# Four graph-network layers on one core: the first layer's weighed messages are made by one-hot matmuls beside the mixing, scattered as rows and summed from plain transfers

## The reference

```
src, dst: 53125 edges (25000 both ways and 3125 loops), sorted by dst
xn  = layernorm(x)
# graph part
h   = xn @ W.T + b
agg = segment_sum(edge_weight[:, None] * h[dst], src, 3125)
x  += elu(agg)
# mixing part
q, k, v = xn @ Wq + bq, xn @ Wk + bk, xn @ Wv + bv     # 8 heads of 32
kv, k_sum = sum over nodes of phi(k) v, phi(k)          # phi(t) = t + 1 or exp(t)
out = (phi(q) kv / (phi(q) k_sum + 1e-6)) @ Wo + bo
y   = layernorm(xn + out) * g1 + b1n
x  += layernorm(y + relu(y @ W1 + b1) @ W2 + b2) * g2 + b2n
```

## Time and profile before

| | us |
|---|---|
| three executions | 5759.25, 5759.92, 5763.4 |
| profiled execution, its span (the page gives no other time for it) | 6101.2 |
| span less the median of the timed executions | 341 |
| from the start to the ELU of the first layer, in the profiled execution | 1508 |
| PE, DVE, POOL, ACT busy over the span | 4335.5, 3233.1, 2977.7, 1242.5 |

### The profile page before, as it was taken

How to read it: one execution, slowest core, us unless ns; L and a number is a source line. 1 busy time by engine, 2 the same in 40 slices (tenths; PEclk the granted TensorE clock), 3 DMA queues, 4 the chain that set the end, 5 groups by cost and what they waited for, 6 DMA issues and landing times. The chain is left out here.

```text
span 6101.2 us, 68061 instructions
## 1 busy us (share of the span) xinstructions
PE 4335.5 (71%) x17944; PEld 3114.6 (51%) x17944; DVE 3233.1 (53%) x7722; ACT 1242.5 (20%) x3067; POOL 2977.7 (49%) x2938
## 2 busy tenths in 40 slices
PE   0298855555987677763985957888489996777764
PEld 0246543333676454432454845566367774566554
DVE  6324544445111666776985155788732224567752
ACT  0022210000322211110123321100033333333221
POOL 1446666665021388873873536676200005666434
PEclk9988876566988776565996977888789998988867
DMA  5100013333211599885743234444300003222234
GB/s 157 39 19 2 2 39 92 91 91 75 91 35 51 163 291 294 273 270 144 240 129 101 73 106 108 111 111 111 75 8 0 0 2 105 79 85 87 65 108 123
DMA packets 402554, 617.08 MB, mean 101 GB/s; under 512 B 79785, under 2 KB 293694, under 8 KB 401829
## 3 DMA queue, kind: packets, MB, share of 16 engines
q0 software_dynamic: 127136, 331.96, 19.3%
q1 hardware_dynamic: 271940, 278.07, 14.5%
q10 hardware_dynamic: 3154, 3.20, 0.2%
HBM read 482.93 MB, written 130.68 MB: 101 GB/s over the span
## 5 line engine op out<-in xcount | busy, mean ns | idle before, releaser
L877 POOL DMA_INDIRECT m_rows<-support,far_at x440 | 447.7, 1018 | 991.7 <-POOLq L126 744.5
L3966 POOL DMA_INDIRECT g_sp_rows<-h,src_at x440 | 466.7, 1061 | 215.9 <-issue 102.1
L3340 POOL DMA_INDIRECT g_sc_rows<-keyval,src_at x440 | 441.6, 1004 | 248.1 <-POOLq L126 109.3
L532 POOL DMA_INDIRECT records<-record,place_at x416 | 416.3, 1001 | 283.6 <-issue 120.4
L877 POOL DMA_INDIRECT g_sums_rows<-h,far_at x440 | 417.0, 948 | 229.8 <-issue 86.8
L3363 PE MATMUL g_sc_pair<-g1q_parts,g_sc_near 125*128 x1320 | 316.3, 367 | 187.4 <-DVE g_sc_rows L3407 137.3
L888 PE MATMUL g_sums_bank<-g_sums_rows,g_sums_same 128*125 128x256 f32 x440 | 217.5, 590 | 286.2 <-issue 251.6
L4015 PE MATMUL g_sp_bank<-g_sp_rows,g_sp_same 128*125 128x264 f32 x880 | 301.0, 449 | 80.9 <-DVE g_total L4155 43.8
L923 DVE TENSOR_TENSOR g_total<-g_total,g_sums_bank 125x256 f32 x440 | 183.4, 417 | 329.1 <-remote 178.5
L949 PE MATMUL m_half<-m_rows,m_marks 128*125 128x256 f32 x880 | 255.2, 425 | 118.4 <-issue 81.2
L987 DVE TENSOR_TENSOR g_total<-g_total,m_half 125x256 f32 x440 | 184.6, 420 | 239.2 <-PE m_half L949 131.4
(11 more groups left out here) (734 smaller groups left out, 10605.8 us busy)
## 6 DMA issues: line engine op xcount, KB each, us to landing
kept<-g_sc_rows SPq DMA_DIRECT2D x440, 128.0 KB
g_sp_rows<-kept SPq DMA_DIRECT2D x440, 128.0 KB
answer_rows<-zero SPq DMA_DIRECT2D x1, 14592.0 KB
g_sc_kind_in<-kind_rows SPq DMA_DIRECT2D x55, 256.0 KB
g_sc_local_in<-local_rows SPq DMA_DIRECT2D x55, 250.0 KB
g_sp_local_in<-local_rows SPq DMA_DIRECT2D x55, 250.0 KB
sorted_rows<-xw SPq DMA_DIRECT2D x15, 640.0 KB
f_W<-answer_rows SPq DMA_DIRECT2D x75, 128.0 KB
```

Of the source, the lines that this page charges most:

```text
L532: nc.gpsimd.indirect_dma_start(core.records, bass.IndirectOffsetOnAxis(ap=core.place_at[:, t:t + 1], axis=0), core.record[:, t, :], None). ...
L877: nc.gpsimd.indirect_dma_start(self.rows[:, k, :], None, self.table, bass.IndirectOffsetOnAxis(ap=core.far_at[:, s:s + 1], axis=0)).then_i ...
L3340: nc.gpsimd.indirect_dma_start(rows[:, k, :], None, table, bass.IndirectOffsetOnAxis(ap=core.src_at[:, s:s + 1], axis=0)).then_inc(gathere ...
L3966: nc.gpsimd.indirect_dma_start(self.rows[:, k, :], None, self.table, bass.IndirectOffsetOnAxis(ap=core.src_at[:, s:s + 1], axis=0)).then_i ...
```

## The change

1. `source_plan`, `RecordPlacing`, `project`, `arrange_records` and `Sums` go. `edge_plan` also fetches the weights by dst (16 gathers in place of 12) and keeps dst and weight in `core.edge`.
2. One phase, `gnn0_front`, does the layer norm, the projection and the places. h is not stored: it stays in SBUF as three bf16 parts whose sum is h (`far_parts`). The places are computed from the arrangement by dst, bucket by bucket, between the tiles of the norm, and summed over the buckets on PE.
3. In `mix0` the class `Messages` makes the messages. For every step PE multiplies a one-hot matrix of the local dst with the three parts of the step's tile (3 bf16 matmuls of 256 columns), ACT copies the product from PSUM with the edge weight as its scale, and POOL scatters the 128 rows of 260 numbers (256, and dst, local src and weight as tags) to their places in DRAM. Before that POOL scatters 25 blocks of zero rows to the places that stay empty. The steps are dealt out over the slots by an estimate of PE's work in each (37 for a kv tile, and so on).
4. For that, two PSUM banks go to the messages: o shares a bank with ctx, t with q, and nd has one bank in place of two, so that the second read waits for the division of the first. The buffers of the queries are one (`joined`).
5. The clearing of the two tables moves into `mix0`, on SP's queue behind the 14th load of `local_in`.
6. `message_sums` loads the messages by plain DMAs of 4 steps, compares the tags with a ramp for 8 steps at once, multiplies and adds. POOL copies the tags out for the fourth layer.
7. The five biases of the mixing become three stacked bf16 rows each, so that one bf16 matmul of 3 partitions adds them.

```diff
+class Messages:
+    SLOTS, TAGGED, NEAR = 12, 4, 2
...
+    def load(self, sp, g):
+        core = self.core
+        if g:
+            sp.wait_ge(self.near_set, g)
+        mine = slice(g * GROUP * W, (g + 1) * GROUP * W)
+        sp.dma_start(self.local_in[:], core.local_rows[mine].partition_broadcast(P)).then_inc(self.marked, 16)
+    def fill(self, pool):
+        nc, core = self.core.nc, self.core
+        for t in range(NT):
+            nc.gpsimd.indirect_dma_start(core.messages, bass.IndirectOffsetOnAxis(ap=core.fill_at[:, t:t + 1], axis=0), core.zero[:, 0:MESSAGE], None).then_inc(self.filled, 16)
+        pool.wait_ge(self.filled, 16 * NT)
+    def scatter(self, pool):
+        nc, core = self.core.nc, self.core
+        for s in range(STEPS):
+            k = s % self.SLOTS
+            if s % self.TAGGED == 0:
+                pool.wait_ge(self.tagged, s // self.TAGGED + 1)
+            pool.wait_ge(self.weighed, s + 1)
+            nc.gpsimd.indirect_dma_start(core.messages, bass.IndirectOffsetOnAxis(ap=core.place_at[:, s:s + 1], axis=0), self.rows[:, k, :], None).then_inc(self.scattered[k], 16)
+        for k in range(self.SLOTS):
+            pool.wait_ge(self.scattered[k], 16 * ((STEPS - 1 - k) // self.SLOTS + 1))
...
+    def expand(self, pe, s):
+        nc, core = self.core.nc, self.core
+        g, k = s // GROUP, s % GROUP
+        if k == 0:
+            pe.wait_ge(self.near_set, g + 1)
+        if s % 2 == 0 and s >= len(self.halves):
+            pe.wait_ge(self.weighed, s - len(self.halves) + 2)
+        if k == 1 and g + 1 < GROUPS:
+            self.tiles.load(g + 1)
+        tile = self.tiles.at(s)
+        for i in range(3):
+            ins = nc.tensor.matmul(self.halves[s % len(self.halves)], self.near[:, g % self.NEAR, k * W:(k + 1) * W],
+                                   core.far_parts[:, i, bass.ds(tile, 1), :].rearrange("p o d -> p (o d)"), start=i == 0, stop=i == 2)
+        ins.then_inc(self.expanded, 1)
+    def weigh(self, act, s):
+        nc, core, k = self.core.nc, self.core, s % self.SLOTS
+        if s % self.TAGGED == 0:
+            if s >= self.SLOTS:
+                for j in range(k, k + self.TAGGED):
+                    act.wait_ge(self.scattered[j], 16 * (s // self.SLOTS))
+            else:
+                act.wait_ge(self.cleared, 1)
+            nc.scalar.activation(self.rows[:, k:k + self.TAGGED, D:D + TAG], core.edge[:, :, s:s + self.TAGGED].rearrange("p r s -> p s r"), ACT.Copy).then_inc(self.tagged, 1)
+        if s % 2 == 0:
+            act.wait_ge(self.expanded, s + 2)
+        nc.scalar.activation(self.rows[:, k, 0:D], self.halves[s % len(self.halves)], ACT.Copy, scale=core.near_weight[:, s:s + 1]).then_inc(self.weighed, 1)
...
+    def compare(self, v, g):
+        nc, core = self.core.nc, self.core
+        v.wait_ge(self.marked, 16 * (g + 1))
+        if g >= self.NEAR:
+            v.wait_ge(self.expanded, GROUP * (g - self.NEAR + 1))
+        nc.vector.tensor_scalar(self.near[:, g % self.NEAR, :], self.local_in[:], core.row[0:P, 0:1], None, ALU.is_equal).then_inc(self.near_set, 1)
+    def follow(self, v, s):
+        if s % GROUP == 0 and s // GROUP + self.NEAR - 1 < GROUPS:
+            self.compare(v, s // GROUP + self.NEAR - 1)
+def mix0(core):
...
+            for stage, part, work in (("y", 0, 42), ("y", 1, 41), ("read", 0, 9), ("hidden", 0, 18), ("hidden", 1, 18), ("hidden", 2, 18), ("hidden", 3, 18),
+                                      ("read", 1, 9), ("turn", 0, 10), ("out", 0, 28), ("q", 0, 27)):
+                r = i - behind[stage]
+                if 0 <= r <= LAST and not (stage == "y" and part >= RUNS[r][1]):
+                    slots.append((stage, r, part, work if stage == "y" else work * RUNS[r][1] // 2))
...
+            for g in range(1, GROUPS):
+                messages.load(sp, g)
+                if g == GROUPS // 4:
+                    sp.dma_start(core.sorted_rows.rearrange("(p r) d -> p r d", p=W), bcast_mid(core.zero[:, 0:D], [W, NT, D])).then_inc(emptied, 16)
+                    sp.dma_start(core.answer_rows.rearrange("(p r) d -> p r d", p=W), bcast_mid(core.zero[:, 0:D], [W, EXPERT_STEPS * EXPERT_ROWS // W + 2 * NT, D])).then_inc(emptied, 16)
...
+def message_sums(core, total):
+    CHUNKS, HELD = 6, 3
+    LOAD = 4
...
+                    sp.wait_ge(summed, LOAD * (i - CHUNKS + 1))
+                    sp.wait_ge(noted, LOAD * (i - CHUNKS) // GROUP + 1)
+                sp.dma_start(rows[:, k * LOAD:(k + 1) * LOAD, :], tile_rows(core.messages, LOAD * i, LOAD)).then_inc(landed[k], 16)
...
+                nc.tensor.matmul(halves[s % len(halves)], marks[:, s // GROUP % HELD, s % GROUP, :], rows[:, s % SLOTS, 0:D], start=True, stop=True).then_inc(summed, 1)
...
+                nc.vector.tensor_tensor(marks[:, g % HELD], bcast_mid(core.ramp[:, 1:P + 1], shape), bcast_last(tags(g, 1), shape), ALU.is_equal).then_inc(matched, 1)
...
+                v.wait_ge(added, s)
+                v.wait_ge(summed, s + 1)
+                nc.vector.tensor_tensor(there, there, halves[s % len(halves)].unsqueeze(1), ALU.add).then_inc(added, 1)
```

More of the change, by code:

```diff
@@ L34 @@
 CHUNK = STEPS // 4
[L35 to L36 removed]
+USED = -(-NE // W)
+TAG = 3
+BIASES, BIAS_PARTS = 5, 3
+MESSAGE = D + 4
 EXPERTS = 8
@@ new lines, in gnn0_front @@
+    parts = core.far_parts
+    with Phase(nc, "g0_front") as ph:
+        w, b, rows = ph.sb("w", [128, DC, D]), ph.sb("b", [P, D]), ph.sb("rows", [P, ROWS, D])
+        loaded, cleared, saved, tiles_in, chain_sem = (ph.sem(n) for n in ("loaded", "cleared", "saved", "tiles_in", "chain"))
+        made, kept = ph.sem("made"), ph.sem("kept")
+        rounded = [ph.sem(f"rounded{i}") for i in range(2)]
+        lessened = [ph.sem(f"lessened{i}") for i in range(2)]
+        norm = NormTiles(core, ph, core.xn, [ph.ps(f"turn{k}") for k in range(2)])
+        banks = [ph.ps(f"bank{k}") for k in range(2)]
+        places = Places(core, ph)
+        FOLD = 16
+        bias, bias_parts = ph.sb("bias", [BIASES * FOLD, D // FOLD]), ph.sb("bias_parts", [BIASES * FOLD, BIAS_PARTS, D // FOLD], BF16)
+        bias_in, bias_set = ph.sem("bias_in"), ph.sem("bias_set")
@@ L461, in _ @@
         @block.tensor
         def _(pe):
-            pe.wait_ge(counted, 1)
-            nc.tensor.matmul(early_bank[:, 0:BUCKETS], earlier[:], count[:], start=True, stop=True)
-            nc.tensor.matmul(total_bank[:, 0:BUCKETS], ones[:], count[:], start=True, stop=True).then_inc(summed, 1)
-            pe.wait_ge(tiled, 1)
-            nc.tensor.transpose(tile_bank[0:4, 0:CHUNK], tile[:], core.ident[0:CHUNK, 0:CHUNK]).then_inc(turned_done, 1)
+            for i in range(NT + 1):
+                if i < NT:
+                    norm.turn(pe, i)
+                t = i - 1
+                if t < 0:
+                    continue
+                if t == 0:
+                    pe.wait_ge(loaded, 32)
+                pe.wait_ge(norm.columns_kept, t + 1)
+                if t >= 2:
+                    pe.wait_ge(kept, t - 1)
+                for c in range(DC):
+                    ins = nc.tensor.matmul(banks[t % 2][0:P, 0:D], core.xnT[:, c, columns(t)], w[:, c, :], start=c == 0, stop=c == DC - 1)
+                ins.then_inc(made, 1)
@@ new lines, in _ @@
+            places.sum_pe(pe)
+            places.assign_pe(pe)
+        @block.scalar
+        def _(act):
+            norm.act_begin(act)
+            for i in range(NT + LAG + 1):
+                norm.act_turn(act, i)
+                t = i - 3
+                if 0 <= t < NT:
+                    act.wait_ge(kept, t + 1)
+                    nc.scalar.activation(parts[:, 0, t, :], rows[:, t % ROWS, :], ACT.Copy).then_inc(rounded[0], 1)
+                t = i - 4
+                if 0 <= t < NT:
+                    act.wait_ge(lessened[0], t + 1)
+                    nc.scalar.activation(parts[:, 1, t, :], rows[:, t % ROWS, :], ACT.Copy).then_inc(rounded[1], 1)
@@ L541, in layer_norm @@
-def layer_norm(core, name, buf, out, outT=None, rows=True, token_affine=None, feature_affine=None, add_to_x=False, add_xn=False, ready=None, placing=None):
+            link = Chain(v, chain_sem).link
+            v.wait_ge(x_in, 32)
+            norm.dve_begin(v, link)
+            places.begin(v, link)
+            v.wait_ge(bias_in, 16 * BIASES)
+            for i in range(BIAS_PARTS):
+                ins = nc.vector.tensor_copy(bias_parts[:, i, :], bias[:])
+                if i < BIAS_PARTS - 1:
+                    link(ins)
+                    link(nc.vector.tensor_tensor(bias[:], bias[:], bias_parts[:, i, :], ALU.subtract))
@@ L544, in layer_norm @@
+            places.spread(v, link)
+            for bucket in range(NT):
+                places.assign(v, bucket)
+            places.tiles(v, link)
+            places.keep(v, link)
+            v.wait_ge(lessened[1], NT)
+def layer_norm(core, name, buf, out, outT=None, rows=True, token_affine=None, feature_affine=None, add_to_x=False, add_xn=False):
```

(3 more changed lines are left out.)

719 lines of the change are left out of this document (311 added, 408 removed).

## The result

The changed kernel takes 5554.32 us (four runs, 5551.59 to 5559.94) against 5759.59 for the kernel before: a ratio of 0.9647 (0.9633 to 0.9661), 205 us faster. The forecast of 5450 was right in its sign and 104 us too low; the time lies inside the range of 5360 to 5590.

What follows compares the result with a forecast made beforehand. It took POOL's gathers to bound the sums, PE and its waits the mixing, one engine's chain the front. 12 + 78 + 135 + 645 + 300 = 1170 against 1508 us, scaled by 0.944, gave 5450 (5360 to 5590).

Steps and rivals of the forecast that it cites:

- the conversion: Whole kernel: 338 us saved in profiled time, scaled evenly by 0.944 to 319, giving 5441; 9 given back makes 5450.
- Edge plan: Phase before the joined front: 78 us (70 to 90) with four more gathers, the source plan's 120 us gone.
- Joined front: Norm, projection and places in one phase: 121 us of DVE work, chains and barrier plus 14 of waits, 135.
- Mixing, POOL: Mixing: POOL's 465 indirect DMAs and their issue, with small additions, form a chain of 596 us; whole mixing 645 (590 to 760).
- The clearing: Mixing, around step 88: the load queued behind the clearing on SP comes late and stops the engines, 40 us taken.
- The fills: Start of the mixing: POOL's 25 fills of zero rows, 32 us, are hardly covered by PE's first messages.
- Mixing, PE: Mixing: PE busy for 566 us with bias matmuls at a quarter of their cost; 650 with its old 84 of waits.
- Sums: Message sums: DVE's 263 us for 440 steps, 12 for the start and 25 for lower clock, 300 (275 to 390).
- PE bounds the mixing: Rival for the mixing, chance 0.18: at a clock of 0.75 PE makes it 758 us, the kernel 5557.
- The sums run at 1.2 GHz: Rival for the sums, chance 0.10: PE at the low clock needs 390 us, the kernel 5535.
- The clearing costs nothing: Rival, chance 0.17: no loss from the clearing in the mixing and sums of 280 us, the kernel 5393.
- Scatters land too slowly: Rival for the mixing, chance 0.05: at 50 GB/s a scatter takes 2.7 us, the mixing 1230, the kernel 5993.

## Why the prediction was right or wrong

The forecast was right in its sign and in most of its mechanism, and missed the size by 104 us, half of what was saved.

*The step that failed* is the conversion: "The profiled span is 6101.2, the median of the runs 5759.92, 0.944 of it; -338 x 0.944 = -319", with 9 us given back. The new stages were built from durations and floors, which hardly differ between the chips; the old ones (1508) held 158 us that the faster chip doesn't have, since its sums end at 1350. So 1170 was set against 1508 x 0.944 = 1424 where 1350 stood. The text had the clue and gave it 9 us: "the 94 us of waits in the old sums may be longer in the profiled execution than in the others". They were 94 there and 11 in the trace of the faster chip; the norm lost 27 more and the mixing 48. Most of the 94, 80 us, was POOL waiting for PE's signals, as told above.

The account is this. With the right end of the old sums the forecast of 1170 would have been a saving of 180 in place of 310, so the conversion cost 130 us. The new stages end at 1150 in place of 1170 (edge plan -7, front -16, mixing +17, sums -14, rounded), which gave 20 back by offsetting errors. That leaves 110, against 104 in the timed executions.

*Edge plan*, 78: measured 71, at the lower end of its range.

*Joined front*, 135: measured 119. DVE was busy for 100.7 of it; its instructions were no shorter than forecast (a scan 1.07 in place of 0.92, an offset 14.8/25 = 0.59 in place of 0.5), but the 14 us for waits in the loop and most of the 24 for small chains were not needed. One term was missed: PE's matmuls that sum the places don't lie beside DVE's offsets, they outlast them. The first two rows are groups by line of the changed kernel's front, the third is from DVE's timeline:

```profile
L517 PE MATMUL g_front_place_bank<-g_front_rank,ident 128*128 128x440 f32 x50 | 21.0, 585 | 2.3 <-DVE g_front_rank L486 2.3
...
L486 DVE SCALAR_TENSOR_TENSOR g_front_rank<-g_front_rank,g_front_first,g_front_member 128x440 f32<-128x440 f32 x25 | 14.8, 670 | 0.0
```

```profile
197.75 0.61 DVE L502 TENSOR_TENSOR place_at<-g_front_place_bank,place_at 128x440 f32<-128x440 f32 x1 [5.42 <-PE g_front_place_bank L517]
```

*Mixing, POOL*: 1.27 us from scatter to scatter as forecast, with a mean of 977 ns. The clearing: 40 taken, 44 to 46 measured, by the load that was named, with DVE stopped before its 15th comparison (step 104, as named) and PE behind 108 steps, not 112: it needed DVE's division earlier than the comparison. *The fills*, "hardly covered": the first scatter stands at 237, 34 us behind the first fill, but ACT's rows are there only at 219, so at most 18 of the 32 us are theirs. The sum of 645 stands against 662. POOL's own chain of 596 stands against 594.

*Mixing, PE*: 566 forecast, 535 measured at a clock of 0.91. The bias matmuls of keys and values went from 682 to 456 ns, not to a quarter. It made no difference here, since POOL's chain was longer than PE's 535 us.

*Sums*: 300 forecast, 286 measured from the first load at 864.6 to the end of DVE's last twelve adds:

```profile
1145.12 5.42 DVE L961 TENSOR_TENSOR g_total<-g_total,g_sums_bank 125x256 f32 x12 [0.42 <-PE g_sums_bank L933]
```

The 25 us for stretches at the lower clock were not needed: PEclk stood at 0.97. The pairing of PE and DVE was missing (0.41 us of idle DVE in eight steps, 23 us).

*The rivals.* "PE bounds the mixing" gave 5557, almost the measured time, and yet by the trace of the faster chip POOL is the bound: the right number from a wrong cause. "The sums run at 1.2 GHz" fell by the clock of 0.97. "The clearing costs nothing" fell by the gap. "Scatters land too slowly" fell too: the last event of a scatter's semaphore stands 1.6 us behind the scatter's end in the median in the changed kernel's trace, beside the clearing 5.6 to 7.2 us, and DMA stood at a share of 0.36 from 440 to 863 us. That ACT waits for the scatters was to be a sign of being wrong, and it does, 162 us in all. But 12 buffers are 15 us of POOL's work, far more than a landing takes: what ACT waits for is POOL's turn, which fits POOL as the bound.

*Open*: why waits for PE end late on the slower chip. On the faster chip no run took work from POOL or from PE, so what bounds the mixing there rests on its trace.

## What to carry to other kernels

Hold the span of a profile against the timed runs before anything is subtracted. If they differ by per cents, don't scale evenly: here the first quarter of the kernel held 46% of the difference, and most of what the old sums lost was waits. Take each old stage once as traced and once at its floor (here POOL's 440 x 1.25 = 550 us for a traced 644), and let both be ends of the range. A long clearing costs what is queued behind it on its own queue; put it where that queue has nothing that is soon wanted. A wait's name in the table is a hint: one false name and one second-hand one stood in these. The semaphore in the code, held against the end of the instruction that raises it, told who was late.

## What was not expected of the hardware

- Chips of two speeds ran the same kernels 6% apart, and unevenly: the changed kernel's sums take 305 us on both, its mixing 662 and 792.
- On the slower ones, waits for PE can end long after the end of the matmul by its record: in the changed kernel's trace 357 of 2257 such waits ended more than 0.5 us behind it (up to 8.4 us for ACT's copies in the mixing), and ahead of each of the 357 stand at least three indirect DMAs of POOL within 15 us. None is in the changed kernel's sums, where POOL issues no indirect DMA, and only one of ACT's waits for a message matmul was late when half of the scatters were left out. In the five traces of the faster chip, with 2185 to 2565 waits for PE each, there is none.
- PE's granted clock, as a mean over a stretch, was 0.62 in the old sums on the faster chip (busy for 399 of 561 us) and 0.97 in the new ones (225 of 279), for the same products. It was 0.79 in place of 0.85 when a third of its matmuls were taken out of the mixing: less work didn't raise it.
- A run of 25 DVE instructions of 0.59 us with two operands in SBUF held one indirect DMA of POOL for 11.44 us, as one long instruction did in the earlier trace rows; two earlier ones went through in the same run.
